# A recommender tower on one core: product matmuls in phases of two and three bank pairs, and new start times for the gathers

## What is computed

```python
e = jnp.stack([tbl_0[ids[:, 0]], ..., tbl_39[ids[:, 39]]], axis=1)   # (2048, 40, 32)
xi, xj = e[:, iidx, :], e[:, jidx, :]                                # the 780 pairs i < j
z = jnp.einsum('bpd,pde,bpe->bp', xi, bilinear_matrices, xj)         # (2048, 780)
h = jnp.concatenate([z, dense_ctx], axis=1)                          # 780 + 16 features
h = jnp.maximum(h @ W_top1 + b_top1, 0.0)                            # 512
h = jnp.maximum(h @ W_top2 + b_top2, 0.0)                            # 256
y = h @ W_top3
```

## Time and profile before

| | |
|---|---|
| time, median of 3 runs (926.9 to 931.82) | 931.17 us |
| the profiled execution, its time | 922.78 us |
| its span (first to last instruction) | 921.0 us |
| TensorE busy | 782.5 us (85%) |
| VectorE busy | 552.8 us (60%) |
| GpSimd busy | 467.1 us (51%) |
| ScalarE busy | 179.0 us (19%) |
| granted TensorE clock, mean share of full | 0.944 |

### The profile page before, as it was taken

One profiled execution on the slowest core, in us unless ns is written; L12 is line 12 of the kernel. 1 busy time (PEld: TensorE's weight loads), 2 busy tenths in 40 slices (PEclk: granted clock), 3 DMA queues, 4 the chain that ended last, 5 costly groups with the idle time before them and its releaser, 6 DMA issues.

```text
span 921.0 us, 24807 instructions
## 1 busy us (share of the span) xinstructions
PE 782.5 (85%) x11178; PEld 445.0 (48%) x11178; DVE 552.8 (60%) x661; ACT 179.0 (19%) x438; POOL 467.1 (51%) x502
## 2 busy tenths in 40 slices
PE   6377931789999899999999988999898999889998
PEld 4244510445555455545454455455454554445556
DVE  6275610566667776766566666666566665456780
ACT  4321200121112211221112311132112301132112
POOL 6554476365544565455544555455544555445200
PEclk8798955899999999999999999999999999989999
DMA  3121211140000100010000100010000000000000
GB/s 107 35 82 27 78 20 25 46 122 12 12 12 9 47 13 11 10 45 13 12 10 11 46 11 12 11 46 12 10 11 11 12 12 11 9 11 12 8 2 0
DMA packets 28291, 23.19 MB, mean 25 GB/s; under 512 B 11754, under 2 KB 24474, under 8 KB 28186
## 3 DMA queue, kind: packets, MB, share of 16 engines
q0 software_dynamic: 15616, 8.03, 6.4%
q1 hardware_dynamic: 11954, 13.08, 4.8%
q10 hardware_dynamic: 616, 0.51, 0.2%
HBM read 21.53 MB, written 0.05 MB: 23 GB/s over the span
## 4 chain that ended last, share of the span: by engine, by line
PE 70%; another core or an unknown queue 14%; issue 10%; ACT 5%; DVE 0%; POOL 0%; ACTq 0%; POOLq 0%; DVEq 0%
PE Y L723 23%; PE ZH L742 22%; PE ZH L768 13%; PE ZH L697 6%; ACT xcols L846 3%; PE ZH L660 2%; PE Y L678 1%; PE Y L777 1%; ACT z L869 1%; PE Y L651 1%; ACT h L873 1%; PE Y L786 0%; PE ZH L777 0%; ACT y L877 0%
## 5 line engine op out<-in xcount | busy, mean ns | idle before, releaser
L615 POOL DMA_INDIRECT rows<-tbl,idx x488 | 465.6, 954 | 393.6 <-PE Y L723 233.6
L988 DVE TENSOR_TENSOR prod<-Y,xcols 128x1024 f32<-128x1024 f32 x336 | 396.4, 1220 | 282.6 <-PE Y L723 192.2
L723 PE MATMUL Y<-xcols,mats 32*128 32x256 f32 (+1 forms) x3712 | 287.2, 404 | 39.8 <-ACT xcols L846 20.4
L742 PE MATMUL ZH<-prod,sel 128*32 128x256 f32 x3200 | 269.8, 394 | 31.3 <-issue 9.6
L723 PEld LDWEIGHTS Y<-xcols,mats 32*128 32x128 f32 (+1 forms) x3712 | 176.2, 173 | 153.7 <-issue 135.7
L742 PEld LDWEIGHTS ZH<-prod,sel 128*32 128x32 f32 x3200 | 102.3, 110 | 146.8 <-issue 111.4
L846 ACT ACTIVATE xcols<-ZH 32x256 f32<-32x256 f32 (+3 forms) x219 | 82.5, 377 | 353.5 <-PE ZH L660 179.2
L768 PE MATMUL ZH<-z,w_sb 128*32 128x256 f32 x1568 | 124.2, 389 | 3.1 <-issue 2.6
L697 PE MATMUL ZH<-one,parts 125*32 125x256 bf16 x1668 | 70.8, 285 | 44.1 <-issue 42.4
L869 ACT ACTIVATE z<-ZH 128x256 f32<-128x256 f32 x56 | 21.5, 384 | 356.9 <-PE ZH L768 205.8
L768 PEld LDWEIGHTS ZH<-z,w_sb 128*32 128x32 f32 x1568 | 62.4, 112 | 37.7 <-issue 11.7
(11 more groups left out here) (48 smaller groups left out, 141.3 us busy)
## 6 DMA issues: line engine op xcount, KB each, us to landing
rows<-tbl,idx POOLq DMA_INDIRECT x488
idb<-ids_turned SPq DMA_DIRECT2D x21, 256.0 KB
mats<-m_wide SPq DMA_DIRECT2D x16, 192.0 KB, 2.9
w_sb<-w SPq DMA_DIRECT2D x7, 256.0 KB
tab<-tbl SPq DMA_DIRECT2D x6, 112.0 KB
w_sb<-w SPq DMA_DIRECT2D x1, 512.0 KB
tab<-tbl ACTq DMA_DIRECT2D x4, 112.0 KB
mats<-m_wide SPq DMA_DIRECT2D x5, 64.0 KB
```

Source lines behind the costliest of these rows:

```text
L615: pool.indirect_dma_start(out=rows[:, slot, t, D * q:D * (q + 1)], out_offset=None, in_=tables[f], in_offset=bass.IndirectOffsetOnAxis(ap= ...
L723: last = pe.matmul(Y[p0:p1, bank, cols], mats[D * r:D * (r + 1), u * P + p0:u * P + p1], xcols[D * r:D * (r + 1), n % 2, UNITS[u][1], :], ...
L742: last = pe.matmul(Z[D * q:D * (q + 1), :], sel[:, GF * (SPAN - 1 - o):GF * (SPAN - 1 - o) + 32], prod[:, (2 * s + bank_of(k, q) // 2) % P ...
L988: dve.tensor_tensor(prod[:, half, :, :].rearrange("p b (u c) -> p b u c", c=BLK), Y[:, pair:pair + 2, :].rearrange("p b (u c) -> p b u c", ...
```

## The change

Four things change together.

1. **Phases.** The unit of work becomes a pair of banks, of which a block has PAIRS = 50. TensorE multiplies two, three and three pairs in a run (`PHASES`, 19 in a block), then does the items of the steps that end there, then the sums of the phase before, with the layer pieces behind each second pair. A tile of z now holds eight pairs, and a pair is one term of its sum (before, a slot was). There are six product buffers (PROD = 6).
2. **Even plan.** Gathers from block 1 on start at step 14 (FREE_UNTIL) and are spread evenly between there and 2.5 steps (LANDS_IN) before their turn. Their starts are 14.39, 14.77, 15.16, ..., and later about 0.40 steps apart.
3. **No gates in block 0.** All 56 gathers of block 0 are sent without waiting for steps or for the head.
4. **Opening.** DVE makes five one-hot operands instead of ten before the first remainder of a table (`rest`), and the ids and the fifth remainder come ahead of step 0; ACT makes the seventh cast earlier; the second head look-up runs place by place instead of part by part. Half of the waits among one-hot operands go, and `idf` gets memory that `y` uses later.

`ITEMS`, the steps at which one-hot operands are made, the matmuls of products and sums and their sizes are as before.

```diff
@@ constants and phases
+PAIRS = 2 * NS
+ZT = -(-PAIRS // SPAN)
+PHASES = [[p for p in part if p < PAIRS] for t in range(0, PAIRS, SPAN)
+          for part in (range(t, t + 2), range(t + 2, t + 5), range(t + 5, t + 8)) if part[0] < PAIRS]
+PHASE_OF = {p: f for f, part in enumerate(PHASES) for p in part}
+def steps_in(f):
+    return [w for w in range(NS) if (PHASE_OF[2 * w + 2] - 1 if w < NS - 1 else len(PHASES) - 1) == f]
-PROD = 4
+PROD = 6
-GATHER_EVERY, LANDS_IN = 0.43, 3.0
-FREE_WAVES = 3
+GATHER_EVERY, LANDS_IN = 0.43, 2.5
+FREE_UNTIL = 14
@@ gather_steps
         if (n, j) == (1, 0):
-            t = 0.0
...
+            t = float(FREE_UNTIL)
+        for _ in range(BT * len(cold(n)[j])):
+            if n == 0:
+                t = -1.0
             else:
-                free = turned[("turn", *waves[k - RING])]
-                t = max(t + GATHER_EVERY, free + 0.5)
+                every = min((turned["turn", *waves[m]] - LANDS_IN - t) / (last[m] - len(at)) for m in range(k, len(waves)))
+                t = max(t + min(every, GATHER_EVERY), turned["turn", *waves[k - RING]] + 0.5)
@@ gather (POOL)
                         if start >= 0:
                             pool.wait_ge(s_y, int(2 * start) + 1)
-                        elif start == -1.0:
-                            pool.wait_ge(s_used, sum(PLACES[h[2]] for h in HEAD if h[0] == "hot"))
@@ multiply (PE)
-            def multiply(n, w):
-                s = n * NS + w
...
-                if s > 1:
-                    pe.wait_ge(s_prod, 2 * s - 2)
-                for pair in range(2):
-                    if pair == 1 and s > 0:
-                        pe.wait_ge(s_prod, 2 * s - 1)
...
+            def multiply(n, p):
+                w, h = divmod(p, 2)
+                g = n * PAIRS + p
...
+                if g >= 3:
+                    pe.wait_ge(s_prod, g - 2)
...
+                last.then_inc(s_y, 1)
@@ add_up (PE)
+            def add_up(n, p):
+                g, tile, o = n * PAIRS + p, p // SPAN, p % SPAN
+                pe.wait_ge(s_prod, g + 1)
+                if o == 0:
...
+                for q in range(QUARTERS):
+                    bank, half = divmod(q, PAIR)
+                    last = pe.matmul(Z[D * q:D * (q + 1), :], sel[:, GF * (SPAN - 1 - o):GF * (SPAN - 1 - o) + 32],
+                                     prod[:, g % PROD, bank, half * BLK:(half + 1) * BLK],
+                                     start=o == 0, stop=o == SPAN - 1 or p == PAIRS - 1, skip_group_check=True)
@@ the order on PE
+            def add_up_phase(n, f):
+                for p in PHASES[f]:
+                    add_up(n, p)
+                    if n > 0 and p % 2 == 1:
+                        mlp(n - 1, *mlp_part(p // 2))
             for n in range(NB):
-                for w in range(NS):
-                    multiply(n, w)
-                    pn, pw = (n, w - 1) if w > 0 else (n - 1, NS - 1)
-                    for what in ITEMS[n * NS + w]:
-                        fill(*what)
+                for f, part in enumerate(PHASES):
+                    for p in part:
+                        multiply(n, p)
+                    for w in steps_in(f):
+                        for what in ITEMS[n * NS + w]:
+                            fill(*what)
+                    pn, pf = (n, f - 1) if f > 0 else (n - 1, len(PHASES) - 1)
                     if pn >= 0:
-                        add_up(pn, pw)
-                        if pn > 0:
-                            mlp(pn - 1, *mlp_part(pw))
+                        add_up_phase(pn, pf)
@@ opening of ACT and DVE
             save_cols(*HEAD[1])
+            cast(*casts[6])
             for what in HEAD[2:]:
                 save_cols(*what)
...
-            cast(*casts[6])
...
-            for v in range(10):
+            for v in range(5):
                 one_hot(v)
             rest(*rests[0])
...
+            dve.wait_ge(s_rest_idx, DMA)
+            ids_fp32()
+            rest(*rests[4])
@@ products (DVE)
-                if h == 0 and s > 1:
-                    dve.wait_ge(s_added, s - 1)
+                if 2 * s + h >= PROD:
+                    dve.wait_ge(s_added, 2 * s + h - PROD + 1)
```

175 lines of the change are left out of this document (83 added, 92 removed).

## The result

The changed kernel takes 1036.88 us (median of 4 runs, 1032.93 to 1049.29), the kernel before 929.03 beside it (923.35 to 931.82). The ratio is 1.115, with a 95% interval of 1.109 to 1.121. 905 us had been forecast. One of the four, 1049.29 us, ran disturbed, at a granted clock of 0.886 against 0.902 to 0.906, and the ratio leaves it out. The profiled execution took 1035.87 us (span 1034.0) against 922.8 before.

A forecast was written before the change was run, and what follows sets the result against it. POOL's unpaused gathers were taken to hold TensorE up, 27 us a block. The terms 54 - 26 - 48 - 13 - 8 + 15 = -26 took 922.8 to 897; keeping the runs' 8.4 us difference gave 905 us, range 872 to 952.

The forecast's parts named there:

- Phases: Blocks 1 to 7: 19 runs instead of 25 save six shape changes there and back per block, -13 us.
- Waits between tiles: Between a tile's last sum and the next tile's first: a third pair of products covers waits for ACT, -8 us.
- the phases stall on products: Rival: a phase's third pair waits for the last product of the phase before, +52 to 957 us; chance 0.21.
- No gates in block 0: Opening: 56 gathers stream to 76 or 77 us and hold the head, step 0 at 82 instead of 28.2, +54 us.
- the hold doesn't last in the opening: Rival: the head gets through by 30 us, five or six steps done by 77 us, -21 to 884; chance 0.16.
- Steps 0 to 14 without gathers: Block 0: with no gather sent in them, these steps take 57 us instead of 83.0, -26 us.
- The long hold: Block 0, steps 15 and 16: the 38 gathers streamed there are spread out, 57.9 us becomes 9.6, -48 us.
- Gathers moved behind: Steady part: 32 more gathers fall there at 0.47 us of hold-up each, +15 us.
- What bounds the kernel: Blocks 2 to 6: work prices sum to 76 us, blocks take 103.1; TensorE is held up 27 us in each.

The follow-up runs named there:

- e3: The changed kernel without the gathers of blocks 2 to 7: 835.74 us, ratio 0.901.
- e6: The changed kernel without the gathers of blocks 2 to 7, only the first item of a phase ahead of the sums from block 1 on: 821.34 us, 0.867.
- e4: The kernel before without the gathers of blocks 2 to 7: 757.61 us, ratio 0.817.
- e14: The changed kernel again, no edit: 767.36 us, ratio 1.129.
- e16: The changed kernel with phases of two pairs only, block 0's gates kept, each gather of blocks 1 to 7 behind its own moment: 679.51 us, 1.000.
- e1: The changed kernel with phases of two pairs each, all else kept: 934.79 us, ratio 1.006.
- e5: The changed kernel without the gathers of blocks 2 to 7, one-hot operands of one column instead of 256 from block 2 on: 829.52 us, no ratio given.
- e7: The kernel before with the even plan of gathers from block 1 on, block 0's gates kept, no phases: 928.24 us, ratio 0.978.
- e8: The kernel before with each gather from block 1 on waiting for its own moment, three in a step: 914.83 us, ratio 0.964.
- e9: The kernel before again, no edit: 679.98 us, ratio 1.000.
- e17: The kernel before with the even plan, block 0's gates kept, each gather of blocks 1 to 7 behind its own moment: 913.28 us, 0.963.
- e2: The changed kernel with the gather plan and gates of the kernel before, phases kept: 1000.54 us, ratio 1.079.
- e12: The changed kernel, gathers of blocks 1 to 7 waiting for a pair's sums instead of its products: 771.33 us, ratio 1.125.
- e13: The kernel before without the gathers of blocks 2 to 7, items and sums between a step's two pairs from block 2 on: 847.76 us, 1.247.

## Why the prediction was wrong

**The step that failed** is *Phases*, "-13 us", where I had "three pairs of products instead of two, 0.44 us more". I took eight records at half of what sixteen take. A pair is half a step by rows of operands, and alone it takes the time of the whole. A run of three pairs takes 1.93 us instead of 1.53. Twelve such runs in a block are 12 x 0.40 = 4.8 us, against 6 x 0.31 = 1.9 saved at changes of shape. Two more parts came with it and weren't in my sum: items back to back on one staging bank (e3's wait of 3.2 us a block, of which e6 gave back 1.8), and the waits for products (1.3). That is 4.8 - 1.9 + 3.2 + 1.3 = 7.4 of the 9.6 us that the phases cost a block (e3 and e4). The rest lies in the three-pair runs as well. Counted in e3's trace from their start to the next start, without their waits, the twelve in a block average 2.09 us and not 1.93: two of them have 40 records, since a step's products are cut in two halves of columns there (2.13 us in e14, 408.63 to 410.76), and a run that stops for a product buffer loses more than its wait (2.23 us beside a wait of 0.60 in e14, 248.47 to 251.30). So they cost 12 x 0.56 = 6.7 us, and the sum is 9.3 of 9.6.

In all, phases were to bring 21 us and cost 84 without the hold (e14 and e16) and 101 under it (the changed kernel and e1). Without its two terms for them the forecast would be 897 + 21 = 918 us; e1, the same kernel without phases of three, took 934.8. So nearly all of the miss is this step.

**Waits between tiles, -8 us.** This part of *Phases* came true, inside the loss. The largest wait of the sums for ACT from 302.2 to 817.6 us before, and the only one left from 312.3 to 924 us in the changed kernel:

```profile
PE ZH L742 <- ACT h L873: 5.2, 6, 0.9
...
PE ZH L761 <- ACT h L899: 0.7, 1, 0.7
```

All waits of the sums for ACT together fell from 11.1 to 0.7 us in blocks 2 to 6. What a phase of three buys there, 2 us a block, is a fifth of what its lone halves and waits cost.

**The rival that ended nearest**, "the phases stall on products" at 957 us, had the right place and the wrong mechanism. The waits for products are 6.4 us in five blocks, not 1.25 us in each of six phases a block, and taking the one-hot operands out of their way left the runs as they were (e5).

**No gates in block 0, +54 us.** The stream of gathers ended where forecast, but step 0 came at 26.1 us, not 82. The head went through beside it, as in the rival "the hold doesn't last in the opening", but this brought almost nothing: that rival counted on five or six steps by 77 us, and there were two. Step 2 came at 85.2 us, as late as step 0 had been forecast (82). In e5 step 0 itself came so late (88.6), and what decides between the two I don't know. The end of block 0 came at 186.5 us against 178 forecast and 198.0 before. e1 without gates and e7 with them end block 0 at 178.7 and 162.6 us: the gates are worth about 16 us, as an estimate, since the two differ in the chip, the opening and the product buffers too.

**Steps 0 to 14 without gathers, -26 us.** The size was right. From step 2 at 85.2 us to step 15 at 143.4 are 58 us (57 forecast), steps 15 and 16 take 13 (10), and steps 17 to 24 take 30 (29).

**The long hold, -48 us.** Right: e7 has only the plan and no pile of due gathers, and its block 0 is 36 us shorter than that of e8 on the same chip. That its cause is gathers is shown by this; that gathers suffice is refuted by e9, where the same code has no such hold.

**Gathers moved behind, +15 us.** The mechanism was right and the term too small. Each gather more in the steady part costs 1.08 to 1.16 us (e17 against e8, e7 against before), not the mean of 0.47. For the 22 more in blocks 2 to 6 (314 against 292) this is 24 us, near my upper end of 30. That it is their number and not their new places is argued.

**What bounds the kernel, 76 us a block and 27 us of hold-up.** Right in both numbers: 76.9 us without gathers (e4). But I had taken the 27 us for the kernel's, and it comes and goes with the chip's condition.

**The rest of the loss.** Under the hold the phases cost more: from e1 (107.9 us a block) to the changed kernel (122.3) it is 14.4 us, from before to e2 9.8, without gathers 9.6. So with the even plan 4 to 5 us a block come on top. A phase raises `s_y` two or three times within 2 us, and the timeline of POOL in the changed kernel shows what follows, from 499.75 us on:

```profile
499.75 0.95 POOL L627 DMA_INDIRECT rows<-tbl,idx  x1 [0.30 <-issue]
501.00 0.95 POOL L627 DMA_INDIRECT rows<-tbl,idx  x1 [0.30 <-issue]
502.25 0.95 POOL L627 DMA_INDIRECT rows<-tbl,idx  x1 [0.30 <-issue]
503.50 0.95 POOL L627 DMA_INDIRECT rows<-tbl,idx  x1 [0.30 <-issue]
506.07 0.95 POOL L627 DMA_INDIRECT rows<-tbl,idx  x1 [1.62 <-remote]
```

At least four in a row. Blocks 2 to 6 of the changed kernel have 48 such runs of four or more, those of e1 have 11. That these runs are the 4 to 5 us is argued, not shown, and one run speaks against it: e2 has 29 of them where the kernel before has 12, at a price of 9.8 us, hardly more than the 9.6 without any gather. e12 was made to test it and ran where gathers held nothing.

**Open** stays what the condition is. The kernel before took 926 to 948 us in three series and 680 in two, once each way on chip 1. The gathers' duration (954 and 964 ns), the busy time of DVE, ACT and POOL and the bytes moved are the same to about 1%; TensorE's busy time is not (782.5 and 646.7 us). The kept traces differ in one thing more, which I count in them and which no view shows: the number of semaphore raises that were recorded. It is 5532 in the kernel before and 11072 in e9, 6145 in the changed kernel and 11243 in e14. Without gathers a block has as many under the hold as without it (281 in block 2 of both e4 and e13); with them, each gather adds about 16 in e9 and about 6 before. So under the hold some 10 raises of each gather are missing from the record. Whether this is a trace of what holds TensorE up, or whether the recording of so many raises is itself the burden, isn't shown: every execution on record has a recorded span and clock, and no experiment here switched the condition on or off.

## What to carry to other kernels

Before a tiled matmul loop is cut into other runs, look which operand rows each piece uses: a piece that fills half of TensorE's row groups costs as much as a whole one when its partner isn't next to it (0.85 us against 0.88 here), so its price is measured on a lone half, never taken as half of a pair. A gain of one semaphore or change of shape for each run (0.31 us here) is soon eaten by that (0.40 us here).

What moves work from a full stretch to a steady one is priced at the margin. Under the hold the mean cost of a gather was 0.45 us, and the next one cost 1.1.

Time the kernel before beside every variant, each time. Here it moved between 680 and 948 us, and a change of 4% under one condition was none under the other; only the phases' loss, 1.115 and 1.129, held in both.

## What the runs showed of the hardware

- Eight product records in two row groups take 0.85 us, sixteen in all four 0.88 (e13).
- With the same program and the same 0.95 us gathers, four blocks took 308.7 us in one series (e9) and five took 515.5 in another, 77 against 103 us each. TensorE's records showed it busy for 306.7 and 471.7 us of these.
- Under the hold each further gather in a steady block made it 1.08 to 1.16 us longer (e17, e7), about what it takes on GpSimd with its pause (1.25 us). All 58 of a block together cost 26 us, 0.45 each (before, e4).
- Without the hold 311 gathers in a row, 1.26 us apart, left TensorE at the 76.7 us a block that it takes without any, until they came too late for their turns (e9).
- The two conditions differ in the semaphore raises recorded, about 6 and about 16 for each gather (before, e9), and both came on the same chip (first and third series).
